# Product keys: gate products of both token halves in turn, in two row groups of the array

## What is computed

```python
xn = (x - mean) * jax.lax.rsqrt(var + EPS) * bn_gamma + bn_beta
q = (xn @ w_q.T).reshape(b, s, 2, NH, KD).transpose(2, 0, 1, 3, 4)
sim = jnp.einsum('pbnhd,hkpd->pbnhk', q, keys_p)
scores, idx = jax.lax.top_k(sim, K)
all_scores = (scores[0][..., :, None] + scores[1][..., None, :]).reshape(b, s, NH, K * K)
all_idx = (idx[0][..., :, None] * NK + idx[1][..., None, :]).reshape(b, s, NH, K * K)
sc, pk = jax.lax.top_k(all_scores, K)
indices = jnp.take_along_axis(all_idx, pk, axis=-1)
hmid = jnp.einsum('bnd,bnhkd->bnhk', inputs, down[indices])
hmid = jax.nn.sigmoid(sc) * jax.nn.gelu(hmid, approximate=False)
return jnp.einsum('bnhk,bnhkd->bnd', hmid, up[indices])
```

## Time and profile before

| | us |
|---|---|
| median of 3 runs | 7446.54 (7446.42 to 7454.33) |
| profiled execution | 7440.85 |
| its span, first to last instruction | 7439.0 |
| TensorE busy / VectorE busy in the span | 6202.7 / 5784.1 |
| product-key stage, first gate build to the end | 5972.7 to 7439 |

### The profile page before, as it was taken

The page is one execution under the profiler, slowest core; times in us unless marked ns, Lnnn a source line. Parts: engine busy times, 40 slices in busy tenths (PEclk is TensorE's granted clock), DMA queues, the critical chain, the costliest instruction groups (busy, mean ns, idle before and its releaser), DMA issues. The chain is left out here.

```text
span 7439.0 us, 185174 instructions
## 1 busy us (share of the span) xinstructions
PE 6202.7 (83%) x76196; PEld 4530.6 (61%) x76196; DVE 5784.1 (78%) x10537; ACT 3453.0 (46%) x7490; POOL 3111.7 (42%) x1651
## 2 busy tenths in 40 slices
PE   6455555599996789999999999997878699999999
PEld 4445554477775655555555555554555488888888
DVE  8899999555546769999999999997565477777775
ACT  4333333233332367777777777774444311111111
POOL 1000000111110049999999999997122122222222
PEclk8767777799998899999999999998889799999999
DMA  3211111201102330211202112111111100000000
GB/s 99 62 38 47 45 40 37 67 31 41 39 14 85 119 102 20 63 39 40 56 28 57 37 40 56 40 39 40 39 50 41 74 6 7 8 7 8 8 7 6
DMA packets 385855, 312.95 MB, mean 42 GB/s; under 512 B 169443, under 2 KB 354790, under 8 KB 384646
## 3 DMA queue, kind: packets, MB, share of 16 engines
q1 hardware_dynamic: 382566, 300.75, 13.8%
q10 hardware_dynamic: 2464, 0.26, 0.0%
HBM read 193.93 MB, written 106.95 MB: 40 GB/s over the span
## 5 line engine op out<-in xcount | busy, mean ns | idle before, releaser
L1865 POOL TENSOR_TENSOR ss_ch<-ss_h,ss_c_all 128x1024 f32<-128x1024 f32 x1024 | 2401.1, 2395 | 161.3 <-DVE ss_h L1888 126.4
L1888 DVE TENSOR_TENSOR_SCAN ss_h<-ss_decay,banks 128x1024 f32<-128x1024 f32 x1024 | 2259.8, 2268 | 169.1 <-PE banks L1785 164.6
L1785 PE MATMUL banks<-ss_diag,ss_dxT 128*32 128x256 f32 x32768 | 1985.3, 383 | 85.8 <-ACT ss_diag L1835 71.7
L1785 PEld LDWEIGHTS banks<-ss_diag,ss_dxT 128*32 128x32 f32 x32768 | 1003.0, 110 | 895.6 <-DVE ss_h L1888 263.1
L1844 ACT ACTIVATE ss_decay<-ss_dt,ss_neg_a 128x510 f32<-128x510 f32 x2048 | 1359.9, 711 | 299.0 <-DVE ss_h L1888 292.8
L627 PE MATMUL banks<-ms_rprod,ident 128*128 128x128 f32 x2048 | 466.9, 400 | 509.6 <-DVE ms_rprod L713 509.6
L2190 POOL TENSOR_TENSOR pk_blockhot<-pk_onehot,pk_parts 128x2048 bf16<-128x2048 bf16 x96 | 345.4, 3626 | 1100.0 <-DVE pk_parts L2428 1100.0
L1835 ACT ACTIVATE ss_diag<-ident,ss_bT 128x128 f32<-128x128 f32 x2048 | 694.9, 387 | 224.5 <-PE banks L1785 215.1
L627 PEld LDWEIGHTS banks<-ms_rprod,ident 128*128 128x128 f32 x2048 | 431.9, 263 | 539.4 <-DVE ms_rprod L713 475.7
L1792 PE MATMUL banks<-ss_ch,ss_stacked 128*32 128x256 f32 x8192 | 639.4, 383 | 80.1 <-POOL ss_ch L1865 80.1
L1047 DVE TENSOR_REDUCE l_nmax<-banks 128x2 f32<-128x512 f32 (+1 forms) x512 | 318.2, 621 | 342.4 <-PE banks L1032 340.8
(11 more groups left out here) (295 smaller groups left out, 9593.4 us busy)
## 6 DMA issues: line engine op xcount, KB each, us to landing
ss_c_all<-keep_cn SPq DMA_DIRECT2D x512, 64.0 KB, 2.1
ss_dt<-keep_dt SPq DMA_DIRECT2D x256, 128.0 KB, 3.6
keep_v<-ms_cx_values SPq DMA_DIRECT2D x32, 512.0 KB, 2.8
l_va<-keep_v SPq DMA_DIRECT2D x32, 512.0 KB, 5.3
l_kf<-keep_k SPq DMA_DIRECT2D x32, 256.0 KB, 3.2
keep_x<-l_x SPq DMA_DIRECT2D x32, 256.0 KB, 2.2
keep_xc<-si_xc SPq DMA_DIRECT2D x16, 512.0 KB, 3.9
keep_zs<-si_zs SPq DMA_DIRECT2D x16, 512.0 KB, 4.9
```

Source lines behind the costliest of these rows:

```text
L1785: m = T_.matmul(inp[u % 2][s * CB:(s + 1) * CB, g, :, t * P:(t + 1) * P], inputs[i % 2][0][:, g, t, u * CB:(u + 1) * CB], diag[slot][:, g, ...
L1865: G_.tensor_tensor(whole(ch[u % CHS]), whole(h[u % 4]), whole(c_all[slot]), ALU.mult).then_inc(weighed, 1)
L1888: V.tensor_tensor_scan(whole(h[u % 4]), whole(decay[u % 4]), whole(inp[u % 2]), 0.0, ALU.mult, ALU.add).then_inc(scanned, 1)
```

## The change

`build` works on pairs: pair p holds tokens 16p to 16p+15 of the lower half and the same 16 of the upper half. Their matmuls alternate, one on partitions 0 to 63, the next on partitions 64 to 127, into two banks: 6 and 7 for even pairs, 3 and 4 for odd ones (banks that `evaluate` used earlier in the round, so pair 1 waits for `raised`). There are four pairs in place of eight groups; a gate step now has two VectorE instructions. `match` is split: the scores of the first key half stand after pair 0, those of the second after pair 1. `turn_h` stands after `evaluate` jb 2 instead of jb 3. On VectorE all six look-ups and `place` stand ahead of the first gate; the gates follow, then `spread`.

```diff
-        def build(n, tg):
-            if tg == 0:
+        def build(n, pair):
+
+            if pair == 0:
                 T_.wait_ge(*blocks_ready.at(n))
                 T_.wait_ge(*rows_ready.at(n))
-            if tg > 1:
-                T_.wait_ge(*gated.at(n, tg - 1))
-            to = bank[6 + tg % 2][:, :].rearrange("p (j t) -> p t j", t=per)
+            if pair == 1:
+                T_.wait_ge(*raised.at(n))
+            if pair > 1:
+                T_.wait_ge(*gated.at(n, pair - 1))
             for u in range(per):
-                tok = tg * per + u
-                ps = slice(0, 64) if tok < 64 else slice(64, P)
+                tok = pair * per + u
                 for part in range(3):
-                    m = T_.matmul(to[:, u, :], rowhot[ps, tok % 64, :], blockhot[ps, part, tok % 64, :], start=part == 0, stop=part == 2)
+                    for half, ps in enumerate((slice(0, 64), slice(64, P))):
+                        m = T_.matmul(gates_of(pair, half).rearrange("p j t -> p t j")[:, u, :], rowhot[ps, tok, :], blockhot[ps, part, tok, :],
+                                      start=part == 0, stop=part == 2)
             m.then_inc(built.sem, 1)
...
             if apply is not None:
-                for jb in range(4):
+                for jb in range(3):
                     evaluate(apply, jb)
             if enter is not None:
                 turn_h(enter)
             if apply is not None:
-                for jb in range(4, 8):
+                for jb in range(3, 8):
                     evaluate(apply, jb)
-            if enter is not None:
-                match(enter)
-            if apply is not None:
-                for tg in range(GROUPS):
-                    build(apply, tg)
+            for pair in range(PAIRS):
+                if apply is not None:
+                    build(apply, pair)
+                if enter is not None and pair < 2:
+                    match(enter, pair)
...
-        def gate(n, tg):
-            if tg == 0:
+        def gate(n, pair):
+            if pair == 0:
                 V.wait_ge(*raised.at(n))
-            a = act[:, :, tg * per:(tg + 1) * per]
-            V.wait_ge(*built.at(n, tg + 1))
-            V.tensor_tensor(a, a, bank[6 + tg % 2][:, :].rearrange("p (j t) -> p j t", t=per), ALU.mult).then_inc(gated.sem, 1)
+            V.wait_ge(*built.at(n, pair + 1))
+            for half in range(2):
+                a = act[:, :, half * 64 + pair * per:half * 64 + (pair + 1) * per]
+                m = V.tensor_tensor(a, a, gates_of(pair, half), ALU.mult)
+            m.then_inc(gated.sem, 1)
...
-            for tg in range(GROUPS):
-                if apply is not None:
-                    gate(apply, tg)
-                if choose is not None and tg < 6:
-                    look_up(choose, tg)
+                for step in range(6):
+                    look_up(choose, step)
+                place(choose)
+            if apply is not None:
+                for pair in range(PAIRS):
+                    gate(apply, pair)
             if choose is not None:
-                place(choose)
                 spread(choose)
```

More of the change, by code:

```diff
@@ L2111, in product_keys @@
     per = 512 // EB
-    GROUPS = P // per
+    PAIRS = P // per // 2
     st = Stage(nc, "pk")
@@ L2144, in product_keys @@
     downed, raised = st.mark("downed", 8), st.mark("raised", 8)
-    built, gated = st.mark("gates_built", GROUPS), st.mark("gated", GROUPS)
+    built, gated = st.mark("gates_built", PAIRS), st.mark("gated", PAIRS)
     upped, added = st.mark("upped"), st.mark("added")
@@ L2215, in turn_h, with match @@
             turn(T_, bank[1], h, chip.ident, h_turned.sem, tiles=1)
[L2217 to L2225, removed]
+        def match(n, half):
+            if half == 0:
+                T_.wait_ge(*xn_ready.at(n))
+                if n == 0:
+                    T_.wait_ge(*fold_copied.at(0))
+            elif n:
+                T_.wait_ge(*sim_ready.at(n - 1))
+            project(T_, bank[1 + half], blocks(xn), [wk[:, kt, half * 512:(half + 1) * 512] for kt in range(KC)]
+                    ).then_inc(matched.sem, 1)
         def turn_vals(n):
```

## The result

The changed kernel takes 7287.83 us (median of 4, 7285.74 to 7289.02) against 7450.43 (median of 4, 7446.42 to 7459.52) for the kernel before: ratio 0.978, 95% interval 0.9763 to 0.9797. The forecast was 7263, in a range from 7230 to 7420. The time fell by 163 us where 183 were forecast.

A forecast was written before the change was run, and what follows sets the result against it. TensorE's own queue was taken to set the 47.19 us round. Builds, turns and wait gave -168 us, the clock -15, in total -183, so 7263 us; range 7230 to 7320, or to 7420 for 8 in 10.

The forecast's parts named there:

- Pace of the builds: TensorE's 384 build records a round start 15.0 ns apart with both row groups side by side, saving 5.3 us a round.
- Turns between shapes: Scores between builds make TensorE switch between full and half height four more times, costing 0.47 us a round.
- The wait ahead of `raise_up`: From build end to `raise_up` on TensorE shrinks from 1.78 to 1.38 us, saving 0.40 a round.
- What hides the moved work: Earlier look-ups and `place` on VectorE, `turn_h` and later `take_scores` delay TensorE nowhere; tightest room 0.5 us, at the Sigmoid.
- The sum: Builds -5.3, turns +0.47 and wait -0.40 give -5.25 us a round, -168 us over 32 rounds.
- The clock: Fewer half-clock stretches in `raise_up`, taken as -15 us in all, bounds -34 to +20.
- the first rival: The sequencer can't feed the builds, so issue sets a pace between 15 and 29 ns; 7416 or 7363 us; chance 0.2.

The follow-up runs named there:

- The first experiment: The changed kernel with the 48 matmuls of a pair's lower half first, then the 48 of the upper half, instead of alternating: 7421.03 us.
- The look-up experiment: The changed kernel with two look-ups after each of gate pairs 0, 1 and 2 and `place` behind gate pair 3: 7371.23 us.

## Why the prediction was right, and where it was off

The direction, the size and the mechanism held. Step by step:

- **Pace of the builds.** Forecast 15.0 ns from the eight records around token 64, measured 14.5 within a pair: 384 records save 5.5 us, not 5.3. The first experiment takes this one thing away (with the change of bank, which the earlier trace rows and the windows beside that experiment rule out) and comes out at 7421 (7420 expected).
- **Turns between shapes.** Forecast 0.47. A stall-free round is 45.51 - 40.22 = 5.29 us shorter; with 5.53 from the pace and 0.39 from the wait, the turns cost 0.63. The starts of the records give 0.61: from full to half height 0.09 or 0.10 as forecast, but from half to full 0.21 and not 0.14, since the second record behind the turn is 0.10 late as well. The bounds (0 to 1.0) held. It isn't a pure loss, since the scores between the pairs give 59 us back.
- **The wait ahead of `raise_up`.** Forecast 1.38, measured 1.39.
- **What hides the moved work.** It held in every part: first gate directly behind `place`, no wait for gates ahead of pairs 2 and 3, none on the Sigmoid. The look-up experiment shows what the cover is worth (83 us). I had costed it at nothing, which is right, but hadn't said that without it half of the gain is lost, and with the scores out of the builds too nearly the whole (10 us left of 163).
- **The sum.** 5.25 us a round forecast, 5.29 measured: -169 in 32 rounds.
- **The clock.** Forecast -15. `raise_up` is busy 463.5 us; at 14.08 a round it would be 450.6, so the drops cost 13 in 7 rounds. Before they cost 33 in 20 rounds (483.5 - 450.6): -20. All 7 are among the 14 rounds with a stall, in which TensorE idles twice within a few microseconds. That -15 came so near is in part luck: it stood for nothing more than fewer drops.
- **The term that was missing** is the first rival in small. I held that the sequencer either feeds the fast pace or sets a pace between 15 and 29 ns. It does neither: it feeds 14.5 ns to the end of a block of 256 instructions, and stalls if the next isn't there. With two score blocks between the pairs that is one stall in every third round, and two in each of the last two tiles (and two more ahead of `turn_vals`): 17.8 + 2.1 = 20 us. They are most of the difference between -183 and -163.

Sum for the stage: -169 - 20 + 20 = -169. From the first fold of the keys to the end it is 1369.4 us in the profile after and 1535.5 before: -166. The two profiled executions as a whole differ by only 155 us, since the unchanged stages ahead took 11 us less in the one before; over the twelve profiles here they take 5904 to 5921 us.

The rule of the Trainium skill ("TensorE: Matmul & The Clock Gate", "Wait — 56ns, not 53.3ns?"), no less than 25 ns from start to start, doesn't hold for two row groups in turn: 14.5 ns in the mean of 96 records, 2 to 4 ns between the two row groups.

## What to carry to other kernels

Small matmuls that use half of the rows can run two at a time if neighbours in the queue lie in different row groups. Here they wrote different banks, too; whether they must wasn't tried. Look in the trace of the slow version for a place where the stream changes its group, for it shows the pace beforehand. Then move the work of the next engine out of the way first: here the faster stream alone gave 10 us, with the reordered VectorE 104 (the kernel with both halves of the scores first, 7346.67), and with the scores between the pairs 163. A dense stream of short instructions needs longer ones spread through it, since the supply of instructions has a pace of its own: in the fastest kernels here no more than 192 (96 records and their loads) stand between two longer stretches.

## What the runs showed of the hardware

- Load and matmul pairs of 64 rows, 128 columns and 32 moving columns in bfloat16 start every 29 ns in one row group, with a change of bank or without. In two row groups in turn they start every 14.5 ns in the mean, 2 to 4 ns and 25 to 27 ns apart by turns.
- A change from full to half height costs 0.09 to 0.10 us, one from half to full 0.21.
- TensorE's instructions come in packets of 16384 bytes, 256 instructions, one block ahead. Where they are used faster than they come, the engine idles at the block's end, for 0.2 to 2.0 us, until 1.2 to 1.6 us after the next packet is in, and the profile shows "issue" as the cause. A lasting stream of pairs gets 128 every 3.47 to 4.02 us, 3.72 in the mean, 29.1 ns a pair.
- An idle time of 1.28 us ahead of `turn_vals` was followed by half the clock (1.2 GHz) in 20 of 32 rounds, one of 0.88 us ahead of `raise_up` in 5 of 32 with the slow builds and in none of the stall-free rounds with the fast ones. Which part of this is the idle time and which the density of the builds wasn't tried.
